# Two exponentials ahead of a normalisation, and the first FP4 input group quantised in two parts

## What is computed

```python
h = _layernorm(x) * (1 + ca) + sa
x = x + ga * _L0_attn_ref(h, Wq, Wk, Wv)          # RoPE, tril mask with k=1, softmax
h = _layernorm(x) * (1 + cb) + sb
x = x + gb * _L0_ffn_ref(h, w_gate, w_up, w_down) # three linear layers of FP4-rounded operands
...
x = x + ga * _L1_attn_ref(h, qk, ov)              # causal, scores h qk h^T
x = x + gb * _L1_ffn_ref(...)                     # 8 experts, the 2 best of each token, one shared
```

```python
scale = jnp.max(jnp.abs(xb), axis=-1, keepdims=True) / 6.0
scale = jnp.maximum(scale, jnp.float32(1e-12))
xn = xb / scale
idx = jnp.searchsorted(_MID, jnp.abs(xn))
q = _GRID[idx] * jnp.sign(xn) * scale
```

## Time and profile before

| | us |
|---|---|
| median of 3 runs | 669.61 |
| lowest, highest run | 666.71, 670.39 |
| the profiled execution, its time | 664.82 |
| its span, from the first to the last instruction | 663.0 |
| around the span | 1.8 |
| TensorE busy | 607.0 (92%) |
| VectorE busy | 467.8 (71%) |
| ScalarE busy | 355.3 (54%) |
| GpSimd busy | 247.2 (37%) |
| mean granted clock of TensorE | 0.995 |

### The profile page before, as it was taken

One profiled execution on the slowest core, in us unless ns is written; L12 is line 12 of the kernel. 1 busy time (PEld: TensorE's weight loads), 2 busy tenths in 40 slices (PEclk: granted clock), 3 DMA queues, 4 the chain that ended last, 5 costly groups with the idle time before them and its releaser, 6 DMA issues.

```text
span 663.0 us, 11002 instructions
## 1 busy us (share of the span) xinstructions
PE 607.0 (92%) x3758; PEld 478.1 (72%) x3780; DVE 467.8 (71%) x1265; ACT 355.3 (54%) x740; POOL 247.2 (37%) x305
## 2 busy tenths in 40 slices
PE   7977899988878899999989998978999999999997
PEld 5645677876666777886768787766677888777775
DVE  4867689786797456826658978679756674787765
ACT  3424454565545464554346456565566556666554
POOL 4256565454674322004465636457452100000000
PEclk9989999999999999999989999999999999999999
DMA  8300000000000000000000000020000000000111
GB/s 258 97 0 2 1 1 1 1 0 1 1 0 1 1 1 1 1 1 0 1 1 1 1 1 1 0 61 2 0 2 1 1 1 1 1 1 16 33 33 48
DMA packets 12494, 9.65 MB, mean 15 GB/s; under 512 B 1868, under 2 KB 10904, under 8 KB 12440
## 3 DMA queue, kind: packets, MB, share of 16 engines
q1 hardware_dynamic: 12440, 8.95, 4.5%
HBM read 6.84 MB, written 2.10 MB: 13 GB/s over the span
## 4 chain that ended last, share of the span: by engine, by line
PE 67%; DVE 15%; ACT 9%; POOL 4%; issue 4%; DVEq 0%; ACTq 0%; POOLq 0%
PE ps L1007 14%; PE ps L859 11%; PE ps L985 8%; PE ps L1191 5%; PE ps L799 4%; PE ps L1193 4%; PE ps L1192 4%; ACT xn L1359 2%; PE ps L1033 2%; PE ps L1034 2%; PE ps L1051 2%; PE ps L794 2%; POOL rstd L644 1%; PE ps L879 1%; DVE row_max L1836 1%
## 5 line engine op out<-in xcount | busy, mean ns | idle before, releaser
L1425 ACT ACTIVATE probsT<-ps 128x512 f32<-128x512 f32 (+3 forms) x160 | 85.4, 534 | 159.0 <-PE ps L985 159.0
L1007 PE MATMUL ps<-v_sb,probsT 128*128 128x129 f32 (+1 forms) x1124 | 152.0, 278 | 2.6 <-ACT probsT L1427 2.6
L1007 PEld LDWEIGHTS ps<-v_sb,probsT 128*128 128x128 f32 (+1 forms) x1124 | 137.8, 191 | 7.3 <-ACT probsT L1427 4.0
L1836 DVE TENSOR_REDUCE row_max<-ps 128x1 f32<-128x512 f32 (+2 forms) x144 | 87.4, 619 | 53.2 <-PE ps L867 26.7
L985 PE MATMUL ps<-ident,probs 128*128 128x128 f32 (+1 forms) x562 | 90.6, 277 | 16.1 <-ACT hT L1352 7.8
L985 PEld LDWEIGHTS ps<-ident,probs 128*128 128x128 f32 (+1 forms) x562 | 63.6, 139 | 48.0 <-issue 43.6
L1399 ACT ACTIVATE probs<-ps,neg_max 128x512 f32<-128x512 f32 (+7 forms) x158 | 93.1, 621 | 7.7 <-DVE neg_max L1843 7.0
L683 POOL TENSOR_TENSOR hq<-ha,hp 128x352 f32<-128x352 f32 x32 | 29.9, 935 | 100.9 <-DVE hp L1886 100.9
L859 PE MATMUL ps<-k_high,q_high 128*128 128x512 f32 (+5 forms) x100 | 42.5, 425 | 6.9 <-ACT probs L1399 6.9
L643 POOL TENSOR_SCALAR minus_mean<-mv 128x4 f32<-128x4 f32 (+1 forms) x16 | 3.8, 237 | 105.1 <-DVE veps L1586 104.9
L1858 DVE RECIPROCAL rsum<-ps 128x1 f32<-128x1 f32 x64 | 10.5, 164 | 41.6 <-PE ps L1007 41.2
(11 more groups left out here) (294 smaller groups left out, 1399.1 us busy)
## 6 DMA issues: line engine op xcount, KB each, us to landing
out<-x_sb SPq DMA_DIRECT2D x7, 256.0 KB, 2.3
hT_all<-in_L_wmod SPq DMA_DIRECT2D x2, 384.0 KB, 4.5
x_sb<-in_L_attn_x SPq DMA_DIRECT2D x2, 256.0 KB, 3.8
rope_cos<-table_cos SPq DMA_DIRECT2D x2, 256.0 KB, 4.5
rope_sin<-table_sin SPq DMA_DIRECT2D x2, 256.0 KB, 5.6
x_sb<-in_L_attn_x SPq DMA_DIRECT2D x1, 512.0 KB, 6.1
rope_cos<-table_cos SPq DMA_DIRECT2D x1, 512.0 KB, 7.1
rope_sin<-table_sin SPq DMA_DIRECT2D x1, 512.0 KB, 7.3
```

The costliest lines, as they stand in the source:

```text
L1007: mm = pe.matmul(bank(OUT_AT, 0, V_W), probsT[0:size, n % 4, k * P:(k + 1) * P], v_sb[0:size, j, :], start=(c == 0 and k == 0), stop=(c == ...
L1425: ins = act.activation(probsT[:, n % 4, 0:full], bank(TURN, 0, full), ACT.Copy)
L1836: ins = dve.tensor_reduce(dst, ps[:, start:start + width], AX.X, ALU.max, negate=single)
```

## The change

ScalarE: the two exponentials of slot 5 are issued in slot 4, behind the last copy of slot 4's turned probabilities and ahead of `normalise_1(0)`. VectorE: `fp4_input(0)`, which stood at the end of slot 4, becomes two calls in slot 5, one for the first tile behind `maximum(6, 0)` and one for the other three tiles behind slot 6's last maximum. Both hold in both batches. GpSimd's waits in `xq_scaled` are split to match, and the semaphore `xq_grid` counts two for each group. Groups 1 to 3 are quantised as before.

```diff
+EARLY_EXP_SLOT = GROUP
...
                 def xq_scaled(g):
-                    pool.wait_ge(xq_grid, b * GROUPS + g + 1)
                     if g >= 1:
                         pool.wait_ge(turned, TURN_AT[b, "fp4_rest", g - 1] + 1)
                     for part, (a, z) in enumerate(FP4_PARTS):
                         cols, done = slice(a * P, z * P), b * 4 * GROUPS + 4 * g + 2 * part
+                        pool.wait_ge(xq_grid, 2 * (b * GROUPS + g) + part + 1)
...
-                    if s:
+                    if s and s != EARLY_EXP_SLOT + 1:
                         exp(s, 0)
-                    if n > 1:
-                        exp(s, 1)
+                        if n > 1:
+                            exp(s, 1)
...
                         if c + 2 < n:
                             exp(s, c + 2)
+                        if s == EARLY_EXP_SLOT and c == turns - 1:
+                            exp(s + 1, 0)
+                            exp(s + 1, 1)
                         if c == min(1, turns - 1) and group_at(s, NORM1_SLOT + 1) is not None:
                             normalise_1(group_at(s, NORM1_SLOT + 1))
...
+                def first_fp4_input(part):
+
+                    a, z = FP4_PARTS[part]
+                    dve.wait_ge(h_shifted, len(FP4_PARTS) * b * GROUPS + part + 1)
+                    if b:
+                        dve.wait_ge(xq_ready, 2 * b * GROUPS)
+                    quantise(qa[:, a * P:z * P], qp[:, a * P:z * P], xn[:, 0, a * P:z * P], (z - a) * P // BLOCK,
+                             qs[:, :, a * P // BLOCK:z * P // BLOCK], lambda: None).then_inc(xq_grid, 1)
...
                     if following:
                         maximum(s + 1, 0)
+                    if s == EARLY_EXP_SLOT + 1:
+                        first_fp4_input(0)
...
                     for c in range(1, following):
                         maximum(s + 1, c)
+                    if s == EARLY_EXP_SLOT + 1:
+                        first_fp4_input(1)
...
-                    if group_at(s, FP4_SLOT) is not None:
+                    if group_at(s, FP4_SLOT):
                         fp4_input(group_at(s, FP4_SLOT))
```

More of the change, by code:

```diff
@@ L1890, in scales_used @@
                     def scales_used():
-                        if g:
-                            dve.wait_ge(xq_ready, 2 * (b * GROUPS + g))
+                        dve.wait_ge(xq_ready, 2 * (b * GROUPS + g))
                     dve.wait_ge(h_shifted, len(FP4_PARTS) * (b * GROUPS + g + 1))
-                    quantise(qa[:], qp[:], xn[:, g, :], GROUP * P // BLOCK, qs, scales_used).then_inc(xq_grid, 1)
+                    quantise(qa[:], qp[:], xn[:, g, :], GROUP * P // BLOCK, qs, scales_used).then_inc(xq_grid, 2)
+                def first_fp4_input(part):
[5 more added lines that the diff above has]
+                             qs[:, :, a * P // BLOCK:z * P // BLOCK], lambda: None).then_inc(xq_grid, 1)
                 def combine(n):
```

## The result

The changed kernel takes 661.33 us (median of 4 runs, 661.08 to 662.65), beside 668.16 for the kernel before in 4 runs (666.66 to 670.39): a ratio of 0.990, with a 95% interval of 0.986 to 0.994. The profiled execution took 661.25 us (span 659.5) beside 664.82 before: 3.6 us less, close to the forecast.

The account below looks back on a forecast made before the run. TensorE, busy 607.0 of 663.0 us, was taken as the bound, gaining only where idle stretches close. Gains of 2.15 + 1.64 = 3.8 us off the median 669.61 gave 665.8 us, range 662.8 to 669.3.

Parts of the forecast that it names:

- Exponentials first: ScalarE, slot 5: early exponentials start slot 6's scores 2.58 us earlier in batch 0, 1.61 in batch 1; ceiling 4.19.
- What is late next: Slot 6: exp(6, 0) waits for VectorE's combined maximum, so batch 0 keeps 2.15 of 2.58 us, batch 1 1.64.
- The first part held by GpSimd: VectorE's first quantisation part, batch 0: GpSimd's pieces hold its steps, so it takes 3.57 us instead of 1.48.
- The clock in batch 1: TensorE, 336 to 339 us at clock 0.50: whether it stays up or falls again, the gain stays 1.6 us.
- Rival A: VectorE's first part: nothing is held, 4.2 to 5.8 us gained, 663.8 at its best; chance 0.20.
- Rivals B and C: B: GpSimd's last xq pieces late, 667.6, chance 0.18. C: slots 7 to 9 take the gain back, 669.0, 0.09.
- Rival D: TensorE's clock: each new fall costs 1.5 to 1.7 us, three end at 670.9; chance 0.08.
- The step that failed: Final time: the 3.8 us saving is taken off the three-run median 669.61, giving 665.8 us.
- the sum: Both batches: 2.15 + 1.64 = 3.8 us off the profiled execution's 664.82, to 661.0.

Follow-up runs that it names:

- after_third: The changed kernel run again with no edit: 662.63 us (10 runs), ratio 0.993 to the kernel before.
- parts_only: The changed kernel with slot 5's exponentials back where they were, the quantisation still in two parts: 667.66 us, ratio 0.999 to the kernel before.
- q_low_cleared: The changed kernel with GpSimd's q_low subtraction of group 2 replaced by a memset: 661.25 us, ratio 0.990 to the kernel before.
- after_again: The changed kernel run again with no edit: 662.94 us (8 runs), ratio 0.992 to the kernel before.
- first_tile_first: The changed kernel with slot 5's rotations behind slot 6's combined maximum and GpSimd rounding xq's first tile ahead of q_low: 662.67 us, ratio 0.993.
- exps_only: The kernel before with only slot 5's exponentials issued early, the quantisation in one piece where it was: 669.46 us, ratio 1.003.

## Why the prediction was right in its steps and wrong in its time

- **Exponentials first.** Right: 2.58 and 1.61 us of idle time are gone, and the first matmul stands at 64.73 (forecast 64.71). The copy behind ScalarE's longer queue came at 67.88 (67.86).
- **What is late next.** Right: exp(6, 0) waits for the combined maximum, at 71.83 (71.78), and the scores of slot 7 start at 72.57 (72.51). The gains are 2.18 and 1.70 us (2.15 and 1.64).
- **The first part held by GpSimd.** Right, and shown twice: 3.60 us in the changed kernel's profile (3.31 in after_third's), 1.57 in parts_only, where GpSimd is done, and the mask step goes 1.18, 0.36, 0.23 as q_low goes from 1.32 us to 0.53 to not there. The multiplication is held too, for which the prediction had only weak evidence. By the rule of the Trainium skill (SBUF — State Buffer, Who interferes with whom) it should be, and the reductions not: 0.94 us held and 0.29 free for the multiplication, beside 0.28 and 0.27 for the reduction, so the traces agree. The memset of q_low_cleared still held the mask step a little.
- **The clock in batch 1.** Right as far as it went: the 3 us at 0.50 are gone in the profile after, and the time to the same place is the same as forecast. Without its wait of 1.61 us for exp(5, 0), though, TensorE has two others with a sum of 1.37 us. That the fall went because that wait went is not shown: parts_only keeps the wait and has no fall either, and in after_again the clock falls right behind the two new waits, to 0.57 from 341 to 345 us.
- **Rival A was mis-stated, and the forecast was partly lucky.** It gave 4.2 to 5.8 us for a first part that nothing holds. But the rotations behind it write the buffer that q_low reads, and first_tile_first shows them waiting for it. In the changed kernel q_low ends at 69.60 and the rotation starts at 69.86, so without any holding it could have come at most 0.3 us sooner. The prediction had missed this wait; it named the queue and not the semaphore. So the gain alone could hardly tell a held first part from a free one behind this wait: that the part is held is shown by its durations, and that 2.15 came out so well is in part luck.
- **Rivals B and C didn't come.** ScalarE's rounding in slot 6 of batch 1, at 344.84, has no idle time before it; and of the 3.9 us at the two places 3.6 are left at the end of the profiled execution. **Rival D** didn't come as a slower kernel, but falls did move: the changed kernel's profile has one from 658 us on, and in after_again and after_third the clock is 0.72 from 179 to 185 us, where it is 1.00 in the kernel before.
- **The step that failed** is the last one, "The median of the three runs is 669.61, 4.8 us above it, which the profile doesn't explain; I take the saving off as it stands". The term that was off is the time that the saving is subtracted from. Two of these three runs, 669.61 and 670.39, belong to the upper third of the runs, the one that goes with the fall of the clock in the opening, and the profiled execution lies where only 4 of 100 runs do. The median of 100 runs is 666.9 and the mean 667.7, which less 3.8 is 663.9. The four runs of the changed kernel all fell into its lower group; its 22 have a median of 662.4 and a mean of 663.0. By the means the change saves 4.7 us, 0.7%, of which 3.9 are at the two places. Each kernel has an upper group of its own, so a median of three or four can move by 3 us through which group its runs fall in: two of the four runs of the kernel before lie in its upper group and none of the changed kernel's four does. That accounts for most of what made 3.9 into 6.8. Against the profile's 664.82 the sum was 661.0 and the changed kernel's profile gave 661.25.
- **What stays open.** The 0.8 us between 3.9 and 4.7. Drawing again at random from the 100 and the 22 runs gives a saving of 3.9 to 5.6 us (95%), so there may be nothing to explain. If there is, one candidate is the fall in batch 0's stretch, which one of four profiles of the kernel before has behind the wait of 2.58 us that the change takes away; it costs 1.7 us there (13.90 beside 12.23). The share of runs with a fall in the opening is the same within chance (7 of 22 beside 34 of 100).

## What to carry to other kernels

When two engines' queues cross, price the moved piece at the place where it lands, beside what the other engines do there: six instructions that take 1.6 us alone took 3.6 beside GpSimd, and by the runs each half of this change gained nothing without the other. Look for semaphores too: here the instruction behind the six had to wait for the same piece of GpSimd anyway, so most of the 2 us was not lost time. Before a saving is subtracted from a median, look whether the runs stand in groups: one profile and three runs that differ by 5 us are a reason to widen the range down to the profile's own time less the saving (661.0), which here would have held the result. And a filler of ten small matmuls in the opening emptied the slow group of the runs (0 of 24), at a price of some tenths of a us in the others.

## What was not expected of the hardware

The same matmuls, with the same idle stretches of 0.26 and some 0.57 us between them, got TensorE's clock at 1.00 in one execution and at 0.53 from 11 to 18 us in another; the groups of runs that go with it are 3.6 us apart by their means. The wait of 2.58 us in batch 0 was followed by 1.00 in three profiles of the kernel before and by 0.51 from 69 to 72 us in a fourth. In exps_only pairs of waits of 1.70 and 1.29 us, and of 2.34 and 1.30 us, were followed by 3 us at 0.50 and at 0.55; that kernel, in which a wait was only moved, is about 2 us slower.
